# Attention and output projection one head later, merged transposes and one bias instruction per head in a fused attention and feed-forward layer

## The reference

```python
x = x + layernorm(attention(layernorm(x)))
x = x + layernorm(ffn(layernorm(x)))

# attention: weights are 4-bit codes with one scale per 128 rows
w = (codes - 8) * scale
q, k, v = x @ wq, x @ wk, x @ wv       # 32 query heads, 8 key/value heads, 128 wide
q, k = rope(q), rope(k)
out = softmax(q @ k.T / sqrt(128) + causal_mask) @ v
return out @ wo
# ffn: silu(x @ gate.T * gs) * (x @ up.T * us), then @ down.T * ds, hidden width 1376
```

## Time and profile before

| | |
|---|---|
| median of three runs | 1589.76 us |
| the profiled execution | 1594.79 us |
| its span, first to last instruction | 1593.0 us |
| granted PE clock over the span | 0.978 |
| busy: PE, VectorE, ACT, GpSimd | 90%, 76%, 59%, 57% |
| share of the DMA engines taken by SyncE's queue | 66.1% |

### The profile page before, as it was taken

How to read it: one execution, slowest core, us unless ns; L and a number is a source line. 1 busy time by engine, 2 the same in 40 slices (tenths; PEclk the granted TensorE clock), 3 DMA queues, 4 the chain that set the end, 5 groups by cost and what they waited for, 6 DMA issues and landing times.

```text
span 1593.0 us, 41176 instructions
## 1 busy us (share of the span) xinstructions
PE 1440.8 (90%) x11104; PEld 858.2 (54%) x11104; DVE 1218.2 (76%) x2884; ACT 936.1 (59%) x2198; POOL 914.7 (57%) x642
## 2 busy tenths in 40 slices
PE   5787898999999999998999999988999986999998
PEld 3454555556555555655555555555555553544543
DVE  7766688788878787877887888777878887776744
ACT  2555666667666666676666666666666763422411
POOL 3566676667766776776677667766676763110100
PEclk9999899999999999999999999999999998999999
DMA  7479888878787778877888788778778866010100
GB/s 241 95 154 179 165 161 158 151 153 159 153 154 153 158 156 145 159 158 152 150 161 165 151 150 160 156 150 152 147 161 156 153 140 122 14 53 21 34 27 27
DMA packets 526713, 217.17 MB, mean 136 GB/s; under 512 B 483041, under 2 KB 484801, under 8 KB 526529
## 3 DMA queue, kind: packets, MB, share of 16 engines
q1 hardware_dynamic: 524064, 210.54, 66.1%
q0 software_dynamic: 2464, 4.23, 1.6%
HBM read 55.32 MB, written 4.19 MB: 37 GB/s over the span
## 4 chain that ended last, share of the span: by engine, by line
PE 51%; issue 11%; DMA 10%; SPq 8%; DVE 7%; POOL 6%; ACT 5%; DVEq 1%; POOLq 0%; ACTq 0%
PE ps_p L792 4%; PE ps_p L790 4%; POOL p_lo L508 4%; PE ps_p L791 4%; PE ps_s L1023 4%; PE ps_s L1024 4%; PE ps_p L814 3%; DMA ot_lo<-o_lo 3%; PE ps_p L815 3%; PE ps_o L843 3%; PE ps_o L845 2%; PE ps_o L844 2%; PE ps_p L1037 2%; PE ps_p L1038 2%; PE ps_s L827 2%
## 5 line engine op out<-in xcount | busy, mean ns | idle before, releaser
L508 POOL TENSOR_TENSOR p_lo<-prob,p_hi 128x1280 f16<-128x1280 f32 x128 | 344.3, 2689 | 182.3 <-ACT p_hi L636 170.5
L1114 DVE SCALAR_TENSOR_TENSOR y<-ps_p,wo_scale,y 128x512 f32<-128x512 f32 x512 | 381.3, 746 | 73.9 <-PE ps_p L815 52.2
L627 ACT ACTIVATE prob<-prob,exp_bias 128x512 f32<-128x512 f32 (+3 forms) x512 | 283.3, 554 | 143.5 <-DVE exp_bias L1136 140.6
L843 PE MATMUL ps_o<-v_hi,ffn_w 128*128 128x128 f16 x1280 | 229.3, 223 | 95.2 <-issue 51.2
L1127 DVE CUSTOM_DVE_ANT_0 prob<-ps_s,mask 128x512 f32<-128x512 f32 (+3 forms) x512 | 238.0, 483 | 78.8 <-PE ps_s L829 78.5
L790 PE MATMUL ps_p<-x_hi,w_hi 128*128 128x512 f16 x640 | 244.9, 383 | 2.3 <-DVE x_lo L1082 1.4
L791 PE MATMUL ps_p<-x_lo,w_hi 128*128 128x512 f16 x640 | 244.7, 382 | 0.0
L792 PE MATMUL ps_p<-x_hi,w_lo 128*128 128x512 f16 x640 | 244.6, 382 | 0.0
L644 ACT ACTIVATE o_f<-ps_o,inv_sum 128x128 f32<-128x128 f32 x512 | 145.9, 368 | 150.4 <-PE ps_o L845 150.4
L845 PE MATMUL ps_o<-v_hi,ffn_w 128*128 128x128 f16 x1280 | 230.1, 224 | 0.0
L844 PE MATMUL ps_o<-v_lo,ffn_w 128*128 128x128 f16 x1280 | 229.7, 224 | 0.0
(11 more groups left out here) (100 smaller groups left out, 2929.1 us busy)
## 6 DMA issues: line engine op xcount, KB each, us to landing
swap<-other SPq DMA_DIRECT2D x320, 128.0 KB, 3.1
w_code<-w_codes SPq DMA_DIRECT2D x36, 384.0 KB, 3.7
w_scale<-w_scales SPq DMA_DIRECT2D x36, 384.0 KB, 5.0
o_code<-o_codes SPq DMA_DIRECT2D x35, 256.0 KB, 3.0
swap<-x SPq DMA_DIRECT2D x16, 256.0 KB, 2.9
out<-z SPq DMA_DIRECT2D x16, 256.0 KB, 2.0
ffn_w<-x SPq DMA_DIRECT2D x3, 1024.0 KB, 9.7
ffn_w<-p_hi SPq DMA_TRANSPOSE x128, 3.7
```

The source lines that it names most:

```text
L508: pool.tensor_tensor(p_lo[:, :], prob[:, hp, :], p_hi[:, :], ALU.subtract).then_inc(p_lod, 1)
L627: act.activation(prob[:, hp, a:a + w], prob[:, hp, a:a + w], ACT.Exp, bias=exp_bias[:, hp, i:i + 1], scale=-1.0, accum_out=exp_sum[:, hp, ...
L843: pe.matmul(o, ph, vh, start=(i == ORDER[0] and j == 0), stop=False)
L1114: dve.scalar_tensor_tensor(tile, ps_p[:, bank, :], scale, tile, ALU.mult, ALU.add).then_inc(o_add, 1)
```

## The change

The attention is done two heads after its scores' split instead of one, and the output projection three: `attend(n-2)` and the output tiles of head n-3 in step n. All that belongs to it moves too (`o_norm(n-2)`, `o_low(n-2)`, `turn_o(n-2)`), and V is projected in step h=2, since the V that step h=1 still reads may not be overwritten earlier. The inverse sums get a buffer per head. `o_hi` and `o_lo` lie side by side and are transposed by one DMA. The bias is one instruction over four minima, after the last group; on ACT the four exponentials stand behind the rounding of the pieces (`rope_high`).

```diff
-FULL = (("K", "V"), ("Q0", "Q1"), ("Q2",), ("Q3",))
+FULL = (("K",), ("Q0", "Q1"), ("Q2", "V"), ("Q3",))
-START = ("K", "V", "Q0", "Q1", "Q2", "Q3")
+START = ("K", "Q0", "Q1", "Q2", "V", "Q3")
...
-    return HG * KT * U - 2 * KT
+    return HG * KT * U - 3 * KT
...
                 after(sp, o_ps, (n - 1) * KT)
                 sp.sem_inc(sp_passed)
-                sp.wait_ge(oq_hid, n + 1)
-                sp.sem_inc(sp_passed)
-                sp.dma_start_transpose(ot_hi[:, hp, :, :], o_hi[:, :]).then_inc(ot_hi_in, 16)
                 sp.wait_ge(oq_lod, n + 1)
                 sp.sem_inc(sp_passed)
-                sp.dma_start_transpose(ot_lo[:, hp, :, :], o_lo[:, :]).then_inc(ot_lo_in, 16)
+                sp.dma_start_transpose(ot[:, hp, :, :], flat(o_parts[:, :, :])).then_inc(ot_in, 16)
...
                     turn_p_lo(n, h % 2)
-                    if not (first and h == 0):
-                        turn_o(n - 1, (h - 1) % 2)
+                    if not (first and h < 2):
+                        turn_o(n - 2, h % 2)
...
                     p_low(n, h % 2)
-                    if not (first and h == 0):
-                        o_low(n - 1)
+                    if not (first and h < 2):
+                        o_low(n - 2)
...
-                    act.wait_ge(bias_done, n * NG + g + 1)
+                    act.wait_ge(bias_done, n + 1)
...
-                    if not (first and h == 0):
-                        o_norm(n - 1, (h - 1) % 2)
+                    if not (first and h < 2):
+                        o_norm(n - 2, (h - 2) % HG)
...
-                    if more:
-                        exps(n + 1, (h + 1) % 2, 0)
-                        exps(n + 1, (h + 1) % 2, 1)
                     if first and h == 0:
                         rope_high(0, 0, "Q3")
...
                                 rope_high(V, vpar, piece)
                     if more:
-                        exps(n + 1, (h + 1) % 2, 2)
+                        for g in range(NG):
+                            exps(n + 1, (h + 1) % 2, g)
                         p_high(n + 1, (h + 1) % 2)
...
-                    if h:
-                        attend(n - 1, r, (h - 1) % 2, pieces_before(U - 1) + START.index("V") + 1)
+                    if h > 1:
+                        attend(n - 2, r, h % 2, pieces_before(U - 1) + START.index("V") + 1)
                     elif not first:
-                        attend(n - 1, 1 - r, 1, pieces_before(U - 2) + START.index("V") + 1)
+                        attend(n - 2, 1 - r, h % 2, pieces_before(U - 2) + START.index("V") + 1)
...
-            attend(UNITS * HG - 1, (UNITS - 1) % 2, 1, 0)
+            attend(UNITS * HG - 2, (UNITS - 1) % 2, 0, 0)
             pe.wait_ge(m_xlo, 2)
             pe.wait_ge(y_read, TT)
-            pe.wait_ge(o_add, outs - 2 * KT)
+            pe.wait_ge(o_add, outs - 3 * KT)
             for nt in range(KT):
-                last_output(HG - 2, nt, nt)
-            pe.wait_ge(o_add, outs - 2 * KT + 1)
+                last_output(1, nt, nt)
+            attend(UNITS * HG - 1, (UNITS - 1) % 2, 1, 0)
...
-            def bias(n, hp, g):
-
-                first, count = min(GROUPS[g]), len(GROUPS[g])
-                dve.wait_ge(low_done, n * TT + DONE[g])
+            def bias(n, hp):
+
+                dve.wait_ge(low_done, (n + 1) * TT)
                 dve.sem_inc(dve_passed)
-                dve.tensor_scalar(exp_bias[:, hp, first:first + count], low[:, hp, first:first + count], EXP_UP, None,
-                                  ALU.add).then_inc(bias_done, 1)
+                dve.tensor_scalar(exp_bias[:, hp, :], low[:, hp, :], EXP_UP, None, ALU.add).then_inc(bias_done, 1)
```

More of the change, by code:

```diff
@@ L222, in layer @@
         o_f = sb("o_f", [P, S], F32, att)
[L223 to L226, removed]
+        o_parts = sb("o_parts", [P, 2, S], F16, att)
+        o_hi, o_lo = o_parts[:, 0, :], o_parts[:, 1, :]
+        ot = sb("ot", [P, 2, 2 * TT, P], F16, att)
         cos = sb("cos", [P, S], F32, att)
@@ L510, in o_low @@
             def o_low(n):
-                after(pool, ot_lo_in, 16 * n)
+                after(pool, ot_in, 16 * n)
                 pool.sem_inc(pool_passed)
@@ L515, in o_low @@
                 pool.sem_inc(pool_passed)
-                pool.tensor_tensor(o_lo[:, :], o_f[:, :], o_hi[:, :], ALU.subtract).then_inc(oq_lod, 1)
+                pool.tensor_tensor(o_lo, o_f[:, :], o_hi, ALU.subtract).then_inc(oq_lod, 1)
             def start_rope(piece):
@@ L572, in _ @@
             unit(UNITS - 1, 1, LAST, last=True)
+            o_low(UNITS * HG - 2)
+            power(2 * TT - 1)
             o_low(UNITS * HG - 1)
-            power(2 * TT - 1)
             full = (FT - 1) * P
@@ L673, in _ @@
             o_centre(0)
+            v_high(0, 0, START.index("V") % 2, START.index("V") + 1)
             rope_high(0, 0, "Q1")
@@ L813, in output @@
                 w = flat(by_half(wo)[:, bass.ds((U >> 2) & 1, 1), h, nt * P:(nt + 1) * P])
-                pe.matmul(ps_p[:, bank, :], w, flat(ot_hi[:, hp, :, :]), start=True, stop=False)
-                pe.matmul(ps_p[:, bank, :], w, flat(ot_lo[:, hp, :, :]), start=False, stop=True).then_inc(o_ps, 1)
+                pe.matmul(ps_p[:, bank, :], w, flat(ot[:, hp, 0:TT, :]), start=True, stop=False)
+                pe.matmul(ps_p[:, bank, :], w, flat(ot[:, hp, TT:2 * TT, :]), start=False, stop=True).then_inc(o_ps, 1)
             def scores(n, U, upar, h, g):
@@ L883, in unit @@
                 names = sequence(slots)
-                idle = place(slots, 2, "O0") if first else 0
+                idle = place(slots, 3, "O0") if first else 0
                 def bank_free(e):
@@ L913, in out_tile @@
                 def out_tile(n, h, nt):
-                    if first and h < 2:
+                    if first and h < 3:
                         return
@@ L918, in out_tile @@
                     if nt == 0:
[L919 to L922, removed]
+                        pe.wait_ge(ot_in, 16 * (n - 2))
+                    if h < 3:
+                        output(U - 1, h + 1, (h + 1) % 2, nt, bank_of(r, e))
                     else:
                         if first:
-                            pe.wait_ge(o_cent, h - 1)
-                        elif b == 0 and h == 2 and nt == 0:
+                            pe.wait_ge(o_cent, 1)
+                        elif b == 0 and nt == 0:
                             pe.wait_ge(o_cent, U + HG)
-                        output(U, h - 2, h - 2, nt, bank_of(r, e))
+                        output(U, 0, 0, nt, bank_of(r, e))
                 for h in range(HG):
@@ L1172, in _ @@
                 lows(0, 0, g)
-                bias(0, 0, g)
+            bias(0, 0)
             start_piece(5)
@@ L1238, in out_tile @@
                     before = outs_before(U) + h * KT + nt
-                    if h > 1:
-                        add_output(U, b, h - 2, nt, bank, before)
+                    if h > 2:
+                        add_output(U, b, 0, nt, bank, before)
                     elif not first:
-                        add_output(U - 1, (b - 1) % NB, HG - 2 + h, nt, bank, before)
+                        add_output(U - 1, (b - 1) % NB, h + 1, nt, bank, before)
                 for h in range(HG):
@@ L1250, in unit @@
                             lows(n + 1, hp, g)
-                            bias(n + 1, hp, g)
+                            if g == NG - 1:
+                                bias(n + 1, hp)
                         out_tile(h, g)
-                    invert(n, h % 2)
+                    invert(n, h)
                     if last and h:
@@ L1295, in _ @@
             xn_low(TT - 1, ps_p[:, 1, :])
-            for nt in range(KT):
-                add_last(HG - 1, nt, (nt + 2) % RING)
+            for h in (2, 3):
+                for nt in range(KT):
+                    add_last(h, nt, (nt + 2) % RING)
             dve.wait_ge(sc_cv, 4)
```

41 lines of the change are left out of this document (22 added, 19 removed).

## The result

The changed kernel is slower: 1617.32 us, the median of four runs (1611.34 to 1621.55), against 1590.80 for the kernel before in the same comparison (1585.22 to 1600.39). The ratio is 1.0158, 95% interval 1.0098 to 1.0217. The prediction was 1577 with a range of 1558 to 1603; it had the wrong sign, and the time lies above its range.

What follows compares the result with a forecast made beforehand. The ACT-GpSimd loop, not PE, was taken to set the unit: (38.7 - 39.23) x 28 = -15, start -1, end +3, together -13 from 1594.79, so 1582 for the profiled run and 1577 at the median; range 1558 to 1603 us.

Steps and rivals of the forecast that it cites:

- closed loop: ACT and GpSimd hand work to each other through in-order queues: 7.98 us from p_lo to p_lo in step h=3.
- (a): Attention at n-2: the wait before L843 goes, worth at most 2.75 us a unit, 77 us.
- (d): Merged o transposes: 1.1 us of SyncE's queue freed a head; PE's stall moves from L843 to L814.
- (b): ACT's order: two more exps enter the loop, one-piece step 9.31 us, two-piece step 10.54, unit 38.7 with swap wait.
- the swap wait: In the two-piece step the second rope sum waits for its swapped halves; 0.25 us a unit kept.
- The last rival: Nothing gained: swaps, late transposes and PE's small slack hold the unit at 39.1 to 39.3; 1584 to 1593 us; 21%.
- (c): Biases: 256 of 384 small VectorE instructions go; worth nothing by itself; merged bias could wait 2.6 us behind a p_lo.
- (e): V in step h=2: bias ready at E+4.9, ACT asks at E+5.7 (E: end of p_high(n+1)); narrowly off the loop.
- The slower rival: V's step: late v_hi or a blocked merged bias delays the exps on the loop; unit 39.7, 1606 us; 19%.
- (f): The run's ends: start -1 and end +3 in the sum; bounds for both together -4 to +7.

Runs made afterwards that it cites:

- e2: The changed kernel with the loads of the next weights issued in step h=2 after the o transpose instead of in h=1: 1591.86 us, ratio 0.9998.
- e1: The changed kernel with all four exponentials ahead of rope_high on ACT, the single bias kept: 1577.64 us, ratio 0.9894.
- e10: The changed kernel with all exponentials ahead of rope_high, weight loads moved to h=2 and the down weights' load held until the last o transpose: 1562.12 us.
- e4: The kernel before with o_hi and o_lo transposed by one DMA, nothing else: 1578.18 us, ratio 0.9898.
- e11: e6 with the down weights' load held until the last o transpose, and o transposed by two DMAs again: 1567.85 us, ratio 0.9834.
- e7: e2 with the load of the feed-forward's down weights held until the last o transpose has landed: 1584.46 us, ratio 0.9934.
- e3: The kernel before with the single bias and all four exponentials behind rope_high, the rest as before: 1649.58 us, ratio 1.0351.
- e5: The changed kernel with three biases again and the exponentials of groups 0 and 1 ahead of rope_high: 1574.05 us, ratio 0.9863.
- e6: e5 with the loads of the next weights moved from step h=1 to h=2 on SyncE: 1562.44 us, ratio 0.9791.

## Why the prediction was wrong

**What bounds the kernel: right.** The closed loop between ACT and GpSimd was there, PE's idling was not what a later attention could free, and PE stayed at 36.5 us of work a unit.

**(a) and (d), the stall moves: right in kind.** Waits at the attention went, waits at the output tile came.

**(b), the exps in the loop: right.** 9.31 forecast, 9.29 measured in the three steps with one rope sum on the path.

**(b), the swap wait: this step failed.** I kept 0.25 us a unit, arguing that against the loop the swap's issue moves some 3 us earlier and its use about as much. The issue moved 0.3 us, since it stands in SyncE's queue behind the three loads, and the landing did not move (4.53 us after p_lo, 4.58 before). The use moved 1.4 us, since o_lo no longer waits for o_hi. So between the starts of o_lo and the rope sum there are 2.2 us instead of 1.1, and the wait is 1.1 us a unit where 0.25 stood. The step h=2 took 11.65 instead of 10.79, the unit 39.52 instead of 38.7, and 0.82 x 28 is 23 of the 29 us between the 1582 forecast for the profiled run and its 1611.3. e2 takes that cause away and gets 25 us back. The last rival named swaps, but priced all its delays together at 0.5 us a unit. Between the medians, 1577 forecast and 1617 measured, there are 11 us more: the profiled run of the kernel before lay 5 us above its median, that of the changed kernel 6 below, and no trace tells why.

**(c) and (e), the bias and V's step: right.** The slower rival did not happen here: in the 28 units ACT never waits for exp_bias, which would have been the sign of it. Over 128 biases of width four the group in the changed kernel reads (minimum, median and longest, in ns)

```profile
L1133 DVE TENSOR_SCALAR exp_bias<-low x128: 169/728/1289, 62.0 to 1327.2; 128x4 f32<-128x4 f32 x128
```

and the step h=3 kept its 9.29. The kernel was slower than before for another reason than the one slower case that I priced. The rule of the Trainium skill that I weighed ("SBUF — State Buffer", "Who interferes with whom": whoever comes second is blocked until the other's instruction is over) agrees with the trace, though the 2.6 us did not come up: the bias ends when GpSimd's instruction ends, as in these rows of the changed kernel (GpSimd, then VectorE),

```profile
480.34 2.62 POOL L504 TENSOR_TENSOR p_lo<-prob,p_hi 128x1280 f16<-128x1280 f32 x1 [2.31 <-ACT p_hi L633]
...
481.97 1.01 DVE L1133 TENSOR_SCALAR exp_bias<-low 128x4 f32<-128x4 f32 x1
```

where 0.99 us of p_lo were left. Of 46 biases that met a p_lo in the steady stretch none began less than 1.59 us into it, so 1.05 us was the most; the 1.29 is one that waited for a whole rope sum, as in e1. Why none began earlier is open. It is the kernel's timing and not a limit of the wait: in e10, near its start, one begins 0.4 us into a p_lo and lasts to its end (GpSimd, then VectorE).

```profile
80.12 2.61 POOL L504 TENSOR_TENSOR p_lo<-prob,p_hi 128x1280 f16<-128x1280 f32 x1 [0.57 <-DMA ffn_w<-p_lo]
...
80.51 2.25 DVE L1135 TENSOR_SCALAR exp_bias<-low 128x4 f32<-128x4 f32 x1
```

**(d), the merge: "1.1 us of SyncE's queue freed", with no time of its own.** e4 and e11 give it 12 and 10 us. This error was on the good side.

**(f), the ends: this step failed too.** +3 forecast for the end, +7.5 measured; with the start +8.2, above the +7 that was the bound for both. I looked at y additions and exps and not at what GpSimd issues there: 4.3 us are the down weights' load beside the last transpose (e7). The other 3 are not taken apart. The start gave +0.7 for -1.

**The decision within the change.** By runs: bias and order +59 on the kernel before (e3) and +43 to +47 in the changed one (e5); the merge -12 (e4); the later attention with V's move -4 beyond the merge (e5 against e4, within their intervals), and -16 together with the moved loads (e6 against e4, for which the loads are better left where they are). The range failed with (b): it took the swap wait at its size before as nearly known, while the point at which the loop wants the swaps was being moved.

## What to carry to other kernels

When two in-order queues hand work to each other, compute their closed loop first: an operation put between the two hand-overs is paid in each step, though its engine is busy half of the time. A step that is moved changes when each small transfer is wanted and what it stands behind. Before a wait is taken over from the old trace, list the queue's issues in the new order, with sizes, and set each landing against its new use: a transfer that was just in time stays hidden only as long as something else is late. And try the parts alone: here one part cost 43 us, and without it the change is a gain of 19 (e5).

## What the runs showed of the hardware that I had not expected

- One transpose of 128x1024 beats two of 128x512 by 10 to 12 us over 128 heads, though its issue waits for the second half.
- 1.0 MB of loads issued ahead of four 128 KB swap transfers made GpSimd wait 1.1 us a unit more on the mean, 2.4 us in the step shown; the swaps were in flight for 4.4 us instead of 2.5. A transpose of o beside a 1.3 MB load from GpSimd's queue lands after 7.77 us instead of 3.1.
- 27 of the 28 biases in the steps h=3 of e1 begin within the 0.05 us in which GpSimd goes from o_lo to the rope sum, and each of them ends with that sum, 1.25 to 1.30 us later. That the meeting is so regular because both sides hang on the same loop is my reading, not shown.
- A blocked bias can lose to more than one GpSimd instruction: one in e1 begins at 146.99, 0.37 us before the end of a p_lo, and lasts 2.74 us, over all of the o_lo and the rope sum that follow it.
